# Second attention of a fused two-layer kernel: scores three units ahead instead of four, a PSUM bank of its own for the value projection, weight loads cut into pieces

## What is computed

```python
def _L1_xattn_ref(x, latents, gamma_media, beta_media, gamma_lat, beta_lat, Wq, bq, Wkv, bkv, Wo, bo):
    ...
    xn = _layernorm(x, gamma_media, beta_media)
    ln = _layernorm(latents, gamma_lat, beta_lat)
    q = ln @ Wq + bq
    kv_input = jnp.concatenate([xn, ln], axis=1)        # 512 keys
    kv = kv_input @ Wkv + bkv
    k, v = jnp.split(kv, 2, axis=-1)
    ...
    q = q * DH ** (-0.5)
    sim = jnp.einsum('bhid,bhjd->bhij', q, k)
    attn = jax.nn.softmax(sim, axis=-1)
    out = jnp.einsum('bhij,bhjd->bhid', attn, v)
    out = out.transpose(0, 2, 1, 3).reshape(b, -1, INNER)
    return out @ Wo + bo
```

## Time and profile before

| what | value |
|---|---|
| median of 3 runs | 825.05 us (823.46 to 827.28) |
| the profiled execution, its own time | 822.46 us |
| its span, first to last instruction | 820.7 us |
| PE busy (matmuls) | 750.3 us, 91% |
| DVE busy | 675.8 us, 82% |
| ACT busy | 519.5 us, 63% |
| POOL busy | 264.1 us, 32% |
| mean granted TensorE clock | 0.970 |

### The profile page before, as it was taken

One profiled execution on the slowest core, in us unless ns is written; L12 is line 12 of the kernel. 1 busy time (PEld: TensorE's weight loads), 2 busy tenths in 40 slices (PEclk: granted clock), 3 DMA queues, 4 the chain that ended last, 5 costly groups with the idle time before them and its releaser, 6 DMA issues. The chain is left out here.

```text
span 820.7 us, 14788 instructions
## 1 busy us (share of the span) xinstructions
PE 750.3 (91%) x4888; PEld 596.7 (73%) x4888; DVE 675.8 (82%) x1643; ACT 519.5 (63%) x1103; POOL 264.1 (32%) x375
## 2 busy tenths in 40 slices
PE   5799999998998599999899999999999999985896
PEld 5577777666556487888788888888888888875333
DVE  5678888877887689988988888888888987974597
ACT  5277676665845476667566666766676666653665
POOL 3333333331031042333233323333333322232555
PEclk9599999999999899999999999999999999997799
DMA  4934444322302544343343434344444434342003
GB/s 130 141 121 128 128 131 125 111 61 95 75 1 71 157 72 79 70 78 78 65 78 78 78 64 91 71 84 89 82 83 80 78 65 78 65 84 51 1 1 103
DMA packets 180571, 68.12 MB, mean 83 GB/s; under 512 B 152640, under 2 KB 178816, under 8 KB 180496
## 3 DMA queue, kind: packets, MB, share of 16 engines
q1 hardware_dynamic: 178000, 66.32, 36.2%
q0 software_dynamic: 2496, 0.87, 0.8%
HBM read 17.46 MB, written 2.10 MB: 24 GB/s over the span
## 5 line engine op out<-in xcount | busy, mean ns | idle before, releaser
L1872 ACT ACTIVATE c_pS<-c_pS,c_neg_max 128x512 f32<-128x512 f32 x128 | 84.8, 662 | 117.2 <-DVE c_neg_max L2062 117.2
L1798 POOL CAST c_pT<-c_turned 128x1024 fp32r<-128x1024 f16 x84 | 87.4, 1054 | 175.5 <-PE c_pO L2408 151.0
L2062 DVE TENSOR_REDUCE c_neg_max<-c_pS 128x1 f32<-128x512 f32 x128 | 87.6, 685 | 28.2 <-PE c_pS L2393 28.0
L571 DVE TENSOR_REDUCE a_neg_max<-ab_ps 128x2 f32<-128x512 f32 x128 | 82.5, 685 | 28.4 <-PE ab_ps L818 27.7
L2046 DVE SCALAR_TENSOR_TENSOR c_planes<-c_pS,c_r_sum,c_planes 128x512 f16<-128x512 f32 x128 | 95.1, 743 | 12.1 <-ACT c_planes L1879 12.1
L1879 ACT ACTIVATE c_planes<-c_pS,c_r_sum 128x512 f16<-128x512 f32 x128 | 87.2, 681 | 16.0 <-DMA c_turned<-c_planes 8.0
L2408 PE MATMUL c_pO<-c_pT,c_v_hi 128*128 128x256 f32 x504 | 95.5, 286 | 0.0
L2380 PE MATMUL c_pK<-w_hi,c_kv 128*128 128x512 f32 x248 | 79.1, 400 | 12.1 <-DVE c_k_lo L2030 7.5
L2354 PE MATMUL c_pK<-c_kv,w_hi 128*128 128x512 f32 x248 | 79.4, 401 | 10.7 <-DVE c_v_lo L2041 9.3
L410 ACT ACTIVATE a_probsT<-ab_ps 128x512 f32<-128x512 f32 x128 | 69.4, 595 | 29.8 <-PE ab_ps L831 29.4
L2408 PEld LDWEIGHTS c_pO<-c_pT,c_v_hi 128*128 128x128 f32 x504 | 83.9, 193 | 5.4
(11 more groups left out here) (416 smaller groups left out, 1928.6 us busy)
## 6 DMA issues: line engine op xcount, KB each, us to landing
a_q_stack<-w_hi SPq DMA_DIRECT2D x94, 64.0 KB, 2.6
a_k_stack<-w_hi SPq DMA_DIRECT2D x48, 64.0 KB, 2.7
c_kv<-w_hi SPq DMA_DIRECT2D x42, 64.0 KB, 2.6
s_ctx<-in_ctx_dram SPq DMA_DIRECT2D x8, 256.0 KB, 3.6
x_sb<-in_x_dram SPq DMA_DIRECT2D x8, 256.0 KB, 4.1
ctx_in<-in_ctx_dram SPq DMA_DIRECT2D x8, 256.0 KB, 2.7
out_dram<-x_sb SPq DMA_DIRECT2D x7, 256.0 KB, 2.2
c_turned<-c_planes SPq DMA_TRANSPOSE x86, 3.0
```

The costliest lines, as they stand in the source:

```text
L571: nc.vector.tensor_reduce(neg_max[:, r // 2 % 2, e, r % 2, :], pS[:, e, :, :], AX_X, ALU.max, negate=True).then_inc(s["max"], 1)
L1798: nc.gpsimd.tensor_copy(pT[:, :, :, half], turned[n % 3].rearrange("p (a t) q -> p a t q", a=2)).then_inc(s["cast"], 1)
L1872: nc.scalar.activation(pS[:, u % LEAD, :], pS[:, u % LEAD, :], ACT.Exp, bias=neg_max[:, u % 4:u % 4 + 1], accum_out=sums[:, u % 4:u % 4 + ...
L2062: nc.vector.tensor_reduce(neg_max[:, u % 4:u % 4 + 1], pS[:, u % LEAD, :], AX_X, ALU.max, negate=True).then_inc(s["max"], 1)
```

## The change

`LEAD` is 3 and `pS` has three banks; the bank freed becomes `pV`, which `project_v` and its two readers use. The waits follow: `project_k` waits for the `k_low` before it, `project_v` for the `v_low` before it. In iteration u the engines now work on unit n + 3 (scores, max, exp, divide) and n + 2 (high, low). The two last units of all (14 and 15 of the last batch) put their scores into `pK` and `pV`, which are free by then, through `unit_bank`. The prologue has one unit of scores fewer and the tail one more. SP no longer issues the weight loads first: eight smaller loads stand between the transposes of batches 0 and 1. `down_cast` goes from heads 3 and 4 to heads 1 and 3, `turn_down` from units 9 and 10 to 8 and 10. In the tail, PE's `turn_x3` goes ahead of `out_project(b, 5)`, and `out_turned(5)` with its low part ahead of `high(15)` and `low(15)`.

```diff
-LEAD = 4
+LEAD = 3
...
+        pV = pb("c_pV", [P, 512])
+        def unit_bank(n):
+            return pS[:, n % LEAD, :] if n < U1 * B - 2 else (pK, pV)[n % 2][:, :]
...
-            sp.wait_ge(s["w_lo"], 2)
-            full = (FT - 1) * P
-            for name, dst in (("L1_ffn_w_gate", ffn_w[0]), ("L1_ffn_w_up", ffn_w[1])):
-                sp.dma_start(dst[:, 0:FT - 1, :], a[name][0:full, :].rearrange("(r p) d -> p r d", p=P)).then_inc(s["next"], DMA)
-                sp.dma_start(dst[0:FR, FT - 1, :], a[name][full:FF, :]).then_inc(s["next"], DMA)
-            sp.dma_start(wd_raw[:, :, :], a["L1_ffn_w_down"].rearrange("(c p) n -> p c n", p=P)).then_inc(s["down"], DMA)
...
                     turn_probs(U1 * b + u)
+                    if b == 0 and u == 2:
+                        sp.wait_ge(s["w_lo"], 2)
+                    if b == 0 and u in (2, 3, 4):
+                        gate_up("L1_ffn_w_gate", ffn_w[0], *((0, 2), (2, 5), (5, 6))[u - 2])
+                    if b == 0 and u in (13, 14, 15):
+                        gate_up("L1_ffn_w_up", ffn_w[1], *((0, 2), (2, 5), (5, 6))[u - 13])
+                    if b == 1 and u in (4, 6):
+                        down_half(u // 2 - 2)
...
-                    if b == B - 1 and u in (9, 10):
-                        turn_down(u - 9)
+                    if b == B - 1 and u in (8, 10):
+                        turn_down(u // 2 - 4)
...
-                    if last and i in (3, 4):
-                        down_cast(i - 3)
+                    if last and i in (1, 3):
+                        down_cast(i // 2)
... (ACT, batch)
-                    high(n + 3, u + 3)
-                    exps(n + 4, u + 4)
+                    high(n + 2, u + 2)
+                    exps(n + 3, u + 3)
... (DVE, batch)
-                    unit_max(n + 4, u + 4)
+                    unit_max(n + 3, u + 3)
-                    low(n + 3, u + 3)
+                    low(n + 2, u + 2)
-                    divide(n + 4, u + 4)
+                    divide(n + 3, u + 3)
... (PE)
-                wait(pe, s["lo"], n - LEAD + 1)
+                if n < U1 * B - 2:
+                    wait(pe, s["lo"], n - LEAD + 1)
+                else:
+                    pe.wait_ge(s["v_lo"], 2 * KT * B)
...
                 values(b, 5)
+                turn_x3(b - 1)
                 out_project(b, 5)
-                turn_x3(b - 1)
...
-                    scores(n + 4, g + 2, u + 4)
+                    scores(n + 3, H1 * b + (u + 3) // 2, u + 3)
-                        v_before = (s["v_lo"], g + 4)
+                        v_before = (s["k_lo"], g + 3)
-                        k_before = (s["k_lo"], g + 4)
+                        k_before = (s["v_lo"], g + 4)
```

63 lines of the change are left out of this document (36 added, 27 removed).

## The result

The changed kernel takes 801.07 us (median of 4 runs, 799.08 to 803.86), the kernel before 824.38 us on the same chip (823.46 to 827.28). The ratio is 0.9714, 95% interval 0.9672 to 0.9755. I had predicted 808.5 us within 802 to 817: the direction was right, but the time lies 0.9 us under the range, and the gain of 23.3 us was half as large again as the forecast 15.5. The profiled execution's own time is 799.78 us, 22.7 us less than before.

A forecast was written before the change was run, and what follows sets the result against it. PE was taken to bound middle batches, with losses at the stage's ends and the DMA queue broken at the start. 9.9 + 3.7 + 0 + 1.9 = 15.5 us off 822.46 gave 807.0; 1.5 added: 808.5 us, range 802 to 817.

The forecast's parts named there:

- Start: Start of the stage: with loads out of the transposes' way, DVE's first `oT_lo` comes sooner; 9.9 us gained, bounds 8.9 and 11.4.
- Pieces at nothing: First batches: the eight smaller loads may land transposes 1 to 2.5 us late, priced at nothing, covered by 1.9 us slack.
- The bank: After 317 us: v's own bank removes PE's waits for `v_lo` before `project_k`; 3.7 us gained, bounds 2 and 5.5.
- Depth: Middle batches: one unit less ahead leaves 1.9 us slack from `low` to `values`; cost 0.
- 3 us in all: Bad bound on the cost of one unit less ahead, where DVE, a load or a ctx load is late.
- Tail: Last units: earlier down casts and reordering, with one more unit to hand over; 1.9 us gained, bounds -2 and +4.
- the removed DMA wait is used up by one more unit: Last units: ACT's 4.16 us transpose wait goes, but one more DVE-ACT unit takes its place, leaving only the reordering's gain.
- 0.2 from fewer slow matmuls: Last units: 0.2 us gained from fewer slow matmuls, beside 1.0 for `out_project(5)` and 0.7 for x3 transposes.
- A: Middle: depth lost, PE waits before `values` or for scores in some units; takes 6 us, 814.5 us; chance 0.17.
- C: Most batches: DVE's bias instructions meet POOL's casts; +5 us, 813.5 us; chance 0.1.
- D: Start, bank and tail all at their better bounds: 21 us gained, 803 us; chance 0.14.
- part 2: The forecast's step on a bank of its own for v, after 317 us: 3.7 us gained, bounds 2 and 5.5.

The follow-up runs named there:

- shared_bank: The changed kernel with v projected into k's bank again and the waits of before; depth, loads and tail as changed: 810.73 us.

## Why the prediction was right or wrong

**Start, 9.9 us forecast (8.9 to 11.4): 10.7.** Right, and by the path written down: transposes at once, `values(0)` at 273.75, and the first `oT_lo` 10.4 us after `low(1)`. The first `oT_lo` was forecast at 280.3, counted from a `low(1)` at 269.16; it came at 278.97 with `low(1)` at 268.56, 0.7 us sooner after it. But I laid nearly all of it to the loads. They are worth 7.3 to 7.7 us; 2.0 us is the bank, of which I had named one wait and priced none, and 1.4 are depth and prologue.

**Pieces at nothing: right.** In the changed kernel no matmul of PE shows a wait for a cast, so what they delayed stayed within the slack. As one block the loads cost 3.1 us.

**The bank, 3.7 us forecast (2 to 5.5): 8.0.** This is the step that failed. "Sum after 317 us: 1.2 + 1.05 + 6 x 0.24" takes the brackets of the matmul rows for the price of the waits, and counts eight of them. In batches 1 to 6 the gain was 6.4 us and from there to the tail 1.6; 7.2 of the 8.0 are the bank and 0.8 the shorter bias pair, by shared_bank. The two large terms were right: 1.05 became 1.1 in the pitch, and of the wait at 404.37 (2.85 became 0.96, 1.9 us) the bank gave 1.1, as forecast, and the bias pair the rest. The small ones were wrong. The brackets leave out the part that the modelled end of the matmul ahead covers, and the waits that it covers wholly: each of the six repeating ones was 0.5 us in the pitch and not 0.24, batches 1, 3 and 4 had another of 0.3 that showed no bracket, and the last batch two more of 0.4 and 0.2. The waits of the kernel before from 310 to 735 us, a view that I did not read:

```profile
PEld c_pK L2354 <- DVE c_v_lo L2041: 14.6, 23, 3.3
PE c_pK L2354 <- DVE c_v_lo L2041: 6.7, 9, 2.8
```

I had the second row's nine waits, one of them counted with the start. The first has 23, and the gain of 8.0 us lies between the two. My upper bound of 5.5 came from the same brackets and so was wrong too.

**Depth, 0: right, and for the reason given.** The slack of 1.9 us was near: the changed kernel has 1.7 to 3.3 us from a cast's end to its `values` in most heads. 1.1 us more on that path cost 17 us in the middle, but not on that path: what came late was DVE's `c_kv`. That the bad bound of "3 us in all" was not needed is partly luck, since it did not ask what a disturbance does to DVE.

**Tail, 1.9 us forecast (-2 to +4): 3.0.** Its marks came as walked through: `low(12)` at T+5.8 (forecast 5.8), `low(13)` 8.6 (8.7), `low(14)` 11.4 (11.6), `oT_lo(5)` 11.8 (12.1), `low(15)` 13.2 (13.3), and "the removed DMA wait is used up by one more unit" held too: with the casts at their old places `low(12)` came at 7.1. What I undersized is how much sooner `out_project(5)` starts (1.0 forecast, 1.4 against the kernel before) and the clock behind a hole: "0.2 from fewer slow matmuls".

**The rivals.** A (waits before `values` in the middle) did not come. C, the meeting of bias and cast, came in batch 1 (1.46 us) and in the last batch (1.66), not in most: right as a mechanism, wrong in extent. D, more gained, at 803 us, is what happened, with part 2 alone beyond its bound. Stage 4 gave another 0.4 us that I had not counted, and 10.7 + 8.0 + 3.0 + 0.4 is within 0.6 us of the 22.7 measured, the difference being that the stage began 0.6 us sooner.

## What to carry to other kernels

Where matmuls are pipelined, price a wait of TensorE by the pitch between two equal points of its program, in a unit with the wait and one without. Here the idle time at the matmul rows was the lower end (3.5 us) and that at the weight-load rows the upper one (9.4), with 5.4 us by the pitch; a wait may show in the second alone.

Behind a load in one queue stands everything that is issued after it; here a transpose behind 2.1 MB landed in 7.0 us and not 3.0. Ask of each transfer who waits for it, put those that someone waits for ahead, and cut up the others.

A slack read from a trace holds only while the engines around it keep their times. Before spending it, look at what would run beside what: here DVE is busy 85% of the time, and more or shifted casts of POOL made its instructions longer. What then stopped PE was another product of DVE, `c_kv`, and not the path whose slack had been measured.

## What the hardware did that I had not expected

POOL's casts hold up more of DVE's instructions than those with two inputs. With three casts a `c_kv` cast (one input in SBUF, output in SBUF) takes 991 ns and not 417, and `c_kvn` 1038 and not 406, while the batch-norm statistics stay at 414 ns and the `low` that reads PSUM at 0.74 us. The other half of the split, with two inputs in SBUF, takes 1402 and not 692. The Trainium skill, SBUF — State Buffer, section SBUF: two separate sides, says that VectorE in a 2-port performance mode or with two SBUF inputs and GpSimd exclude each other for a whole instruction; the two-input instructions agree with it, and the one-input ones would by the first half of it, which my prediction left out; no trace here shows the mode of an instruction.

A DMA of 512 bytes and the wait for it took 2.0 us of SP's time, most of what a transpose of 256 KB takes to land (3.0).
